# A sandwich-normed attention and feed-forward block on one core: residual sums, layernorm normalisations and x transposes put into other slots, and shift rows placed by one transfer

## What is computed

```python
x = L0_attn_hidden_states                                   # (16, 512, 512)
x = x + _layernorm(_L0_attn_ref(_layernorm(x), Wq, bq, Wk, bk, Wv, bv, Wo, bo))
x = x + _layernorm(_L0_ffn_ref(_layernorm(x), gate_w, up_w, down_w, gate_s, up_s, down_s))

def _L0_attn_ref(h, ...):                                   # 32 heads of 16 channels
    q, k, v = split_heads(h @ Wq.T + bq), split_heads(h @ Wk.T + bk), split_heads(h @ Wv.T + bv)
    q, k = rope(q), rope(k)
    scores = einsum('bhqd,bhkd->bhqk', q, k) / sqrt(16)     # causal mask, then softmax
    return merge_heads(softmax(scores) @ v) @ Wo.T + bo
```

## Time and profile before

| | |
|---|---|
| median of 3 runs | 2686.7 us (2679.96 to 2687.29) |
| the profiled execution | 2681.5 us |
| its span, first to last instruction | 2679.8 us |
| busy: PE, DVE, ACT, POOL | 2426.6, 1931.4, 1446.7, 1164.6 us |
| mean granted PE clock | 0.972 |
| attention phase | from 0 to about 1655 us of the span |
| in 750 to 850 us | PE busy 95.87, DVE 89.66, ACT 76.06, POOL 73.43 us, clock 1.00 |

### The profile page before, as it was taken

One profiled execution on the slowest core, in us unless ns is written; L12 is line 12 of the kernel. 1 busy time (PEld: TensorE's weight loads), 2 busy tenths in 40 slices (PEclk: granted clock), 3 DMA queues, 4 the chain that ended last, 5 costly groups with the idle time before them and its releaser, 6 DMA issues. The chain is left out here.

```text
span 2679.8 us, 54601 instructions
## 1 busy us (share of the span) xinstructions
PE 2426.6 (91%) x18816; PEld 1134.6 (42%) x18816; DVE 1931.4 (72%) x5887; ACT 1446.7 (54%) x1902; POOL 1164.6 (43%) x1531
## 2 busy tenths in 40 slices
PE   4889999999999999999999973299999999999997
PEld 2434444444444444444444331144444444444443
DVE  5888889889888888988988853645555555555554
ACT  3577777777777777777777661422222222222221
POOL 3566776777776677677677642000000000000000
PEclk8899999999999999999999987699999999999999
DMA  4444445544554554554454434102111111111111
GB/s 163 120 129 141 159 144 158 168 150 151 167 159 143 166 165 145 159 168 151 143 170 142 142 103 181 72 16 79 47 47 47 63 47 47 73 52 47 47 47 48
DMA packets 178934, 305.62 MB, mean 114 GB/s; under 512 B 32416, under 2 KB 115872, under 8 KB 165536
## 3 DMA queue, kind: packets, MB, share of 16 engines
q1 hardware_dynamic: 178720, 302.86, 34.5%
HBM read 182.73 MB, written 119.01 MB: 113 GB/s over the span
## 5 line engine op out<-in xcount | busy, mean ns | idle before, releaser
L753 DVE CUSTOM_DVE_ANT_0 mx<-mx,causal 128x512 f32<-128x512 f32 (+3 forms) x2048 | 942.6, 517 | 69.7 <-PE mx L864 68.9
L587 ACT ACTIVATE probs<-ts,exp_scale 128x1024 f32<-128x1024 f32 x640 | 710.7, 1111 | 166.8 <-PE ts L878 165.8
L1153 ACT ACTIVATE silu<-gu,gate_scale 128x512 f32<-128x512 f32 x176 | 121.0, 688 | 630.9 <-PE gu L1344 630.9
L1128 POOL TENSOR_TENSOR f_rstd<-f_var,f_neg_half 128x4 f32<-128x4 f32 x32 | 32.3, 1010 | 928.7 <-DVE f_var L1271 646.0
L1294 DVE SCALAR_TENSOR_TENSOR hidden<-gu,up_scale,silu 128x512 f32<-128x512 f32 x176 | 131.9, 749 | 416.6 <-PE gu L1344 406.4
L465 POOL TENSOR_SCALAR_AFFINE_SELECT probs<-probs 128x512 f32<-128x512 f32 x512 | 336.9, 681 | 32.9 <-ACT probs L587 32.7
L892 PE MATMUL xb<-probs,vs 128*32 128x512 f32 (+3 forms) x4096 | 306.4, 440 | 13.4 <-ACT shift_rows L593 12.5
L1342 PE MATMUL gu<-f_xT_hi,gate_hi 128*128 128x512 f16 x704 | 267.7, 380 | 52.5 <-issue 52.5
L878 PE MATMUL ts<-qT,kT 64*128 64x512 f16 (+3 forms) x2048 | 246.0, 298 | 52.9 <-ACT probs L587 50.7
L753 DVE DVE_READ_ACCUMULATOR2_ANT row_max<- 128x1 f32 x2048 | 282.8, 138 | 0.0
L1344 PE MATMUL gu<-f_xT_lo,gate_hi 128*128 128x512 f16 x704 | 267.6, 380 | 0.0
(11 more groups left out here) (145 smaller groups left out, 4282.8 us busy)
## 6 DMA issues: line engine op xcount, KB each, us to landing
slots<-half SPq DMA_DIRECT2D x260, 128.0 KB, 13.7
qT<-slots SPq DMA_DIRECT2D x128, 256.0 KB, 3.6
kT<-slots SPq DMA_DIRECT2D x128, 256.0 KB, 3.7
weighed<-oT SPq DMA_DIRECT2D x128, 256.0 KB, 4.5
xn<-x SPq DMA_DIRECT2D x16, 1024.0 KB, 7.4
xr<-x SPq DMA_DIRECT2D x16, 1024.0 KB, 7.8
slots<-half SPq DMA_DIRECT2D x256, 64.0 KB
spread<-recips SPq DMA_DIRECT2D x64, 256.0 KB
```

The costliest lines, as they stand in the source:

```text
L587: nc.scalar.activation(probs[:, g % 2, u, :, :], ts[:, :, :], ACT.Exp, scale=exp_scale[:, 0:1]).then_inc(ts_read, 1)
L753: last = nc.vector.tensor_tensor_reduce(out=scores, in0=scores, in1=causal[:, T - P * (qt + 1):T], scale=1.0, scalar=-3e38, op0=ALU.add, o ...
```

## The change

It moves entries of five tables: two of the four transposes of x go one group later (units 22 and 32 to 27 and 37), the quarters of x are normalised in units 21, 23, 25, 26 (before: 19, 20, 20, 21), those of the projected output in 4, 6, 11, 13 (5, 6, 9, 10), and the residual is added in units 10, 11, 20, 21 (6, 6, 11, 11); the store of x1 goes from unit 14 to 24, the load of xr from 19 to 29. On SP `place_shift` comes directly behind `send_slots`, ahead of `fetch_sums` and `send_recips`, and is one DMA: POOL now writes the shift with the pair of heads innermost, so that the 8 rows arrive in the order of the 4 partitions with 2 pairs each.

```diff
-        shift_rows = sb("shift_rows", [P, 2, T], F16)
+        shift_rows = sb("shift_rows", [8, 2, T], F16)
...
-        TURNED = (("x", 2, 1), ("x", 3, 1), None, None, ("x", 0, 2), None, ("x", 1, 2), None)
+        TURNED = (("x", 2, 1), ("x", 3, 1), None, None, None, ("x", 0, 2), None, ("x", 1, 2))
...
-        NORMALISE_AT = {19: (0,), 20: (1, 2), 21: (3,)}
+        NORMALISE_AT = {21: (0,), 23: (1,), 25: (2,), 26: (3,)}
...
-        NORMALISE1_AT = {5: (0,), 6: (1,), 9: (2,), 10: (3,)}
-        RESIDUAL_AT = {6: (0, 1), 11: (2, 3)}
+        NORMALISE1_AT = {4: (0,), 6: (1,), 11: (2,), 13: (3,)}
+        RESIDUAL_AT = {10: (0,), 11: (1,), 20: (2,), 21: (3,)}
...
-                turned_rows, placed = held(sp, NG * i + g + 1), held(sp, 32 * (NG * i + g))
+                turned_rows, placed = held(sp, NG * i + g + 1), held(sp, 16 * (NG * i + g))
                 sp.wait_ge(shift_read, turned_rows)
                 wait_if_any(sp, shift_in, placed)
-                for pair in range(2):
-                    sp.dma_start(qT[SHIFT_ROWS, g // 2, 2 * (g % 2) + pair, :],
-                                 shift_rows[4 * pair:4 * pair + 4, g % 2, :]).then_inc(shift_in, 16)
+                pairs = slice(2 * (g % 2), 2 * (g % 2) + 2)
+                sp.dma_start(qT[SHIFT_ROWS, g // 2, pairs, :], shift_rows[:, g % 2, :]).then_inc(shift_in, 16)
...
+                    if u == 2 and exists(i + (g + 1) // NG):
+                        place_shift(i + (g + 1) // NG, (g + 1) % NG)
-                    if u == 1 and g in SUMS_AT:
+                    if u == 2 and g in SUMS_AT:
...
-                    if u == 1 and g in FETCHED:
+                    if u == 2 and g in FETCHED:
...
-                    if u == 2 and exists(i + (g + 1) // NG):
-                        place_shift(i + (g + 1) // NG, (g + 1) % NG)
...
-                    if s == 14 and exists(i - 2):
+                    if s == 24 and exists(i - 2):
...
-                    if s == 19 and exists(i - 2) and exists(i - 1):
+                    if s == 29 and exists(i - 2) and exists(i - 1):
...
-                nc.gpsimd.tensor_scalar(shift[:, :, :, :, 0], row_max[:, g % 2, :, :, :], -1.0 / SHIFT_UNIT, None,
+                nc.gpsimd.tensor_scalar(shift[:, :, :, 0, :], row_max[:, g % 2, :, :, :], -1.0 / SHIFT_UNIT, None,
...
-                            op0=ALU.add, op1=ALU.max, accum_out=row_max[:, g % 2, qt, pair, j:j + 1])
+                            op0=ALU.add, op1=ALU.max, accum_out=row_max[:, g % 2, qt, j, pair:pair + 1])
```

More of the change, by code:

```diff
@@ L477, in shift_of_maxima @@
                 pool.wait_ge(shift_step, 2 * (NG * i + g + 1))
-                nc.gpsimd.tensor_tensor(shift[:, :, :, :, 1], row_shift[:, :, :, :], shift[:, :, :, :, 0],
+                nc.gpsimd.tensor_tensor(shift[:, :, :, 1, :], row_shift[:, :, :, :], shift[:, :, :, 0, :],
                                         ALU.subtract).then_inc(shift_ready, 1)
@@ L590, in read_shift @@
             def read_shift(i, g):
-                wait_if_any(act, shift_in, 32 * (NG * i + g - 1))
+                wait_if_any(act, shift_in, 16 * (NG * i + g - 1))
                 act.wait_ge(shift_full, NG * i + g + 1)
-                nc.scalar.activation(shift_rows[0:8, g % 2, :], xb16[0:8, bank_of("s", g), 0:T], ACT.Copy).then_inc(shift_read, 1)
+                nc.scalar.activation(shift_rows[:, g % 2, :], xb16[0:8, bank_of("s", g), 0:T], ACT.Copy).then_inc(shift_read, 1)
             def read_weighed(i, g):
@@ L872, in transposed_scores @@
                 if u == 0:
-                    pe.wait_ge(shift_in, 32 * (NG * i + g + 1))
+                    pe.wait_ge(shift_in, 16 * (NG * i + g + 1))
                 wait_if_any(pe, ts_read, NS * i + n)
```

## The result

The changed kernel takes **2695.6 us** (median of 17 runs, 2685.2 to 2703.5) where the kernel before took 2684.8 on the same chip (17 runs, 2677.5 to 2693.0). The ratio is **1.0042, 95% interval 1.003 to 1.0055**: slower by 0.4%. The prediction said 2659 us, with 2637 to 2681 as its range and 0.07 for slower. It was wrong in sign.

A forecast was written before the change was run, and what follows sets the result against it. PE, busy 91% of the span, was taken as the bound, losing time mostly to waits for ACT. Terms summed to -24.7, from 2681.5 to 2656.8 us; half of the median's 5.2 us excess gave 2659, range 2637 to 2681.

The forecast's parts named there:

- shift rows: SP's one DMA in place of two, issued ahead of sums and reciprocals: an earlier landing taken as worth 0.
- output side: units 9 to 12, and unit 5 to 4: Moved residual sums and output normalisations gain 18 us in units 9 to 12; the normalisation moved to unit 4 costs 5.6.
- transposes one group later: DVE's low half xT_lo moves from unit 34 to 39, delaying unit 2's cosine and PE: 0.5 us in 15 sequences, +7.5.
- x normalised later: Fewer normalisations in units 19 to 22 gain 17 us; one in unit 26, before the shift rows' copy, costs 4.2.
- xr loaded in unit 29: The load follows the store of x1 by five units, some 11 us, as before: no cost.
- other sequences: Waits for ACT beyond sequence 7's rate, 20 us in all: a third taken as gained, -7 us.
- Units 10 to 12, -18: 1.58 us lost to ACT's load, less 0.3 for a later shift-rows copy: 1.3 gained in 14 sequences, -18 us.
- Units 20 to 22, -17: 1.46 us lost to ACT's normalisations, less 0.3 for a later shift-rows copy: about 1.2 gained in 14 sequences.
- "handed on" rival: In units 11 and 21 PE meets POOL's late shift, hanging on DVE's maxima: 0.5 us each, 2680 us; chance 0.17.
- Copy of the shift rows: Sign for right: PE's weighing waits for ACT's copy of the shift rows, rising above 12.5 us in times.
- The list: Closing signs: right if exponential waits fall below 25 us, wrong if units 10 to 12 stay above 8.3 us.
- The slower rival: POOL's residual sums in units 10 and 20 block DVE's low halves: 35 us more, 2694 us; chance 0.07.

The follow-up runs named there:

- e1: Only the new shift layout, its single DMA and SP's new order, put on the kernel before; 2671.9 us, ratio 0.9974.
- e6: The changed kernel with x's normalisations and transposes back at their old units and xr loaded in unit 39; 2662.4 us, ratio 0.9927 to the kernel before.
- e10: e6 with both transposes of x moved to units 27 and 37, nothing else; 2685.9 us, ratio 0.9987 to the kernel before.
- e4: The changed kernel with xr loaded in unit 39 instead of 29, nothing else; 2680.0 us, ratio 0.998 to the kernel before.
- the square above: Four kernels, xr in unit 29 or 39: 1.0042 and 0.998 with x's new normalisations and transposes, 0.9969 and 0.9927 with the old.
- e12: e6 with only the first transpose of x moved, to unit 27; 2669.8 us, ratio 0.9941 to the kernel before.
- e3: Only x's later normalisations and transposes, put on the kernel before; 2697.8 us, ratio 1.0058.

## Why the prediction was wrong, point by point

| term | predicted, us | measured | from |
|---|---|---|---|
| shift rows | 0 | -7 | e1 |
| output side: units 9 to 12, and unit 5 to 4 | -18 + 5.6 | -12.6 | e6 less e1, -0.47% |
| transposes one group later | +7.5 | +16 | e10 less e6, +0.60% |
| x normalised later | -17 + 4.2 | -2 | e4 less e10, -0.07% |
| xr loaded in unit 29 | 0 | +17 | change less e4, +0.62% |
| other sequences | -7 | in the rows above | |
| sum | -24.7 | +11.3 | 1.0042 |

Each measured term is a difference of two medians' ratios times 2685, so it is good to some 6 us. The -2 is not told from 0. e6 has the load of xr in unit 39, where the prediction's output side had it in 29 at no cost. That the output side comes out at -12.6 against -12.4 is partly luck: in the profiles units 20 to 22 lose 0.6 us a sequence more in e6 than in e1, which no term of the prediction foresaw.

- **The load of xr, "five units or some 11 us later, as now: 0".** This is the step that turned the sign: without its 17 us the change stands at 0.998. The rest of the distance to 2659 us is in the transposes (8 us more than predicted), the later normalisations of x (11 us less gained) and the 7 us of the other sequences. I asked whether xr is there in time for its own reader. I did not ask what a 1 MB transfer, 7.9 us to its landing, is put in front of: the slots, for which SP stands in line, and behind them the weighed values, whose buffer ACT must have back. The prediction gave the DMAs of the change no neighbours.
- **The transposes, "from unit 24 to 29 no cosine that PE waits for: 0".** I followed the low half on DVE and not the bank that the table also hands over, though the text says that `BANK_USES` is built from it. The bank put the cost of the late copy into units 38 and 39, 2.08 us a sequence; the square above shows that without it the load costs about as much, in other units. The transposes' own price is the next point. e4 gets 2.0 of the 2.08 back, but loses 0.5 more in units 20 to 22 and 0.5 more in units 0 to 2 and 5 to 7 together, so that its whole loss falls by 1.24 a sequence (7.15 to 5.91), which fits the 17 us.
- **xT_lo to unit 39, +7.5.** The mechanism was right in part, and the term was mis-sized: +16. DVE has no idle time there, and its lateness is PE's. I looked for it at the cosine of unit 2, and it shows in units 0 and 1 as well, where POOL's shift is due. The loss of units 0 to 2 rises by 0.73 us a sequence from e6 to e10, 11 us over 15 sequences, against 0.5 a sequence predicted. Of the 0.73, 0.44 is there in e12 already, without xT_lo in unit 39. There aT_lo is longer, which would do it; that is argued and not shown. The rest of the 16 us lies in units 20 to 22 and 27 to 31.
- **Units 10 to 12, -18.** Right: 1.52 us a sequence gained (1.80 to 0.28) where 1.3 was forecast, and most of the remaining loss is the predicted one by the copy of the shift rows: in sequence 7 the copy ends at 784.79 and the weighing starts at 784.94, 0.2 us late.
- **Units 20 to 22, -17.** Right in size in sequence 7 and most others, where 0.33 us is left, but by luck: PE waits 0.26 of it for POOL's shift in unit 21, and the copy of the shift rows, for which the prediction had set 0.3, holds it no longer in unit 22. That is the "handed on" rival, at half its price. In the mean the gain is 0.8 a sequence, because in sequences 2, 3 and 11 that wait is 1.87 to 1.92 us. These are the three of sequences 2 to 13 in which the averages land latest (POOL takes them up 3.3 to 4.1 us behind the start of unit 16, elsewhere at most 3.04). In sequence 2 POOL works on without a stop from there to the shift, and does not wait for DVE's maxima, as the rival had it. POOL and then PE in sequence 2, units 17 and 21, after:

```profile
313.82 1.28 POOL L483 TENSOR_TENSOR averaged<-averaged,spread 128x512 f32<-128x512 f32 x1 [4.26 <-DMA averaged<-weighed]
...
322.60 0.26 POOL L472 TENSOR_SCALAR shift<-row_max 128x16 f16<-128x16 f32 x1
```

```profile
321.60 0.38 PE L877 MATMUL ts<-qT,kT 64*128 64x512 f16 x2
323.89 0.38 PE L901 MATMUL xb<-ident,shift 128*8 128x128 f16 x4 [1.92 <-POOL shift L477]
```

- **x normalised later, -17 + 4.2 against -2.** From e10 to e4 units 20 to 22 gain 1.1 us a sequence, about what the -17 promised, but units 27 to 31 lose 1.0 more where the 4.2 had 0.3. Of this 0.28 is in unit 27, as predicted. Most of the rest is in units 30 and 31; in unit 31 of 9 of sequences 2 to 13 PE waits 0.34 to 0.48 us for POOL's shift, a wait that had no term.
- **Copy of the shift rows.** The list said that the wait rises above 12.5 us in times. It has more times (19 to 35) and a smaller total (7.9). The long waits of unit 22 (14 of up to 0.87 us before) are gone, and waits of 0.16 to 0.21 us have come in units 7 and 27.
- **Shift rows, 0.** A gain of 7 us, not foreseen; in the changed kernel the wait for their transfer even rises to 5.4 us in 5 waits, which the list named as a wrong sign.
- **The slower rival, sums on POOL against DVE's low halves.** It did not occur as described. The low halves of the roped keys take 0.68 us in unit 11 and at most 0.80 in unit 21, above 1.2 nowhere. The slower side came by another way, which no rival named. The list of signs did not catch it either: units 10 to 12 were not above 8.3 us, the waits for POOL's shift were 17.1 us and not above 25, and only the wait for the shift rows' transfer stood on it.
- **The tail, 0.** It is 4 us longer in the profile. In the other profiles it lies between 47.4 and 52.2 us, in kernels with the new sums as with the old (e3, which has the old ones: 52.0), so the sums do not explain it. Not settled.

## What to carry to other kernels

When a large transfer is given another slot, look at what is issued behind it in the next few microseconds, who waits for those in program order, and which single buffer they return: its own reader may have ample time and the move can still cost 17 us. When an entry of a table moves, follow everything that is built from the table, banks and buffers included, not only the instruction. And where the two halves of a change pull apart, as here, the square of four kernels (with and without each) is cheaper than an argument: it showed a version at 0.9927 next to a change measured at 1.0042.

## What the runs showed of the hardware

DVE's low half of the averages, aT_lo, reads two SBUF tiles, and it took 0.73 us or more everywhere. In the prediction I called an overlap with POOL worth 0.47 us, from 1.21 less 0.74. More rows tell what the overlap costs. The wide POOL operation that ran when aT_lo began, in the kernel before, sequence 7:

```profile
774.26 1.27 POOL L446 TENSOR_TENSOR turned<-biased,sin_sb 64x512 f32<-64x512 f32 x1
```

It ends at 775.53, and aT_lo (774.87, 1.21 long) ends at 776.08, 0.55 later. In e10 the POOL operation beside aT_lo ran to 559.40 and aT_lo to 559.95, again 0.55 later; in e6 to 554.26 and to 554.81, again 0.55:

```profile
558.13 1.27 POOL L452 TENSOR_TENSOR roped<-roped,turned 128x512 f32<-128x512 f32 x1
```

```profile
552.99 1.27 POOL L452 TENSOR_TENSOR roped<-roped,turned 128x512 f32<-128x512 f32 x1
```

So POOL's operation held up DVE's, which then needed 0.55 of its 0.74 us. This is no accident of three cases. In the profiles of before, after, e4, e6, e10 and e12, 162 aT_lo began during a POOL TENSOR_TENSOR (or up to 0.05 us before it) with more than 0.19 us of it to go, and all 162 ended 0.54 to 0.56 us behind its end. The 111 that met one of POOL's maskings so (TENSOR_SCALAR_AFFINE_SELECT on probs) did the same, at 0.54 to 0.55. The price is not a fixed 0.47 but whatever is left of POOL's operation, less 0.19. At worst the two start together. DVE and then POOL in e10, sequence 5, unit 39:

```profile
654.11 1.85 DVE L727 SCALAR_TENSOR_TENSOR aT_lo<-averaged,bias_v,aT_hi 128x512 f16<-128x512 f32 x1 [0.23 <-ACT aT_hi L546]
```

```profile
654.15 1.27 POOL L452 TENSOR_TENSOR roped<-roped,turned 128x512 f32<-128x512 f32 x1
```

DVE's record even starts 0.04 us earlier, and it is DVE that is held, for 1.11 us. It is behind this aT_lo that PE waits 0.43 us for xT_lo above. The prediction read the 0.74 us of unit 19 as a sign that a narrow POOL operation costs nothing; it was 0.74 because that operation ended just as aT_lo began.

The Trainium skill (SBUF — State Buffer, Who interferes with whom) says that a DVE instruction with two SBUF inputs contends with a GpSimd instruction that reads SBUF, and that the one that comes second fully blocks. These rows agree, and the prediction should have followed it in the sizes. It would have looked in the wrong place, though. None of the moved sums met such an operation for long; it is POOL's rope and its masks that meet aT_lo, and in unit 39 they did so for longer once the transposes had moved.
